# Four preactivated layers on 192x192x64: the input's shift and sums spread over three engines, and the weights of later layers prepared in later stages

## The reference, cut to what matters

```python
x = x + L0(gn(x))   # triangle multiplication
x = x + L1(gn(x))   # triangle multiplication
x = x + L2(gn(x))   # MLP with weights and activations rounded to fp8 by rows
x = x + L3(gn(x))   # triangle multiplication, masked
```

```python
h = (x - mu) * rsqrt(var + eps) * ln_w + ln_b
ab = fp8_linear(h, w1); a, b = split(ab)
out = fp8_linear(relu(a) * b, w2)
# fp8_linear: each row of x and of w is divided by max|row|/448 and rounded to fp8, the product is scaled back
```

## Time and profile before

| what | value |
|---|---|
| device time, median of 3 runs | 1818.19 us (1813.92 to 1819.84) |
| device time of the profiled execution | 1815.44 us |
| span of the profiled execution, first to last instruction | 1813.7 us |
| mean granted TensorE clock over the span | 0.913 of full speed |
| busy share of PE, DVE, ACT, POOL | 80%, 83%, 60%, 53% |
| start of the first group norm's reduction | 91.90 us |
| start of the group norm of layer 1, layer 2, layer 3 | 493.34, 898.61, 1440.2 us |

### The profile page before, as it was taken

How to read it: one execution, slowest core, us unless ns; L and a number is a source line. 1 busy time by engine, 2 the same in 40 slices (tenths; PEclk the granted TensorE clock), 3 DMA queues, 4 the chain that set the end, 5 groups by cost and what they waited for, 6 DMA issues and landing times.

```text
span 1813.7 us, 30465 instructions
## 1 busy us (share of the span) xinstructions
PE 1453.9 (80%) x9712; PEld 982.0 (54%) x9712; DVE 1503.7 (83%) x3826; ACT 1095.1 (60%) x2284; POOL 969.2 (53%) x665
## 2 busy tenths in 40 slices
PE   5569998899779997898899846666666489998765
PEld 1146666765456666765587613333333267767654
DVE  6889993398799992399689989999999699981588
ACT  2246662399646562399543367777777267771598
POOL 7378870187588870287555503333333488850354
PEclk8779999899979999899999958889899889999789
DMA  7024435277634435377544304344444434436377
GB/s 258 0 70 112 109 88 134 82 215 206 172 84 106 108 88 136 84 218 194 173 108 112 79 18 111 94 114 97 113 98 110 117 94 107 115 73 150 120 259 248
DMA packets 408831, 225.51 MB, mean 124 GB/s; under 512 B 343456, under 2 KB 343776, under 8 KB 408672
## 3 DMA queue, kind: packets, MB, share of 16 engines
q1 hardware_dynamic: 270240, 185.81, 37.4%
q10 hardware_dynamic: 138432, 37.76, 8.9%
HBM read 114.97 MB, written 66.06 MB: 100 GB/s over the span
## 4 chain that ended last, share of the span: by engine, by line
issue 32%; PE 31%; DVE 14%; ACT 11%; POOL 8%; DMA 3%; SPq 0%; ACTq 0%; POOLq 0%; DVEq 0%
PE ps L1145 11%; ACT work L992 8%; PE ps L1150 7%; PE ps L1106 5%; POOL work L518 4%; PE ps L1135 4%; PE ps L1225 4%; POOL work L472 3%; DMA gate_dram<-work 2%; DVE work L746 2%; ACT work L978 2%; DVE stats L804 2%; DVE work L634 1%; DVE tok L814 1%; DVE pairs L851 1%
## 5 line engine op out<-in xcount | busy, mean ns | idle before, releaser
L512 POOL TENSOR_TENSOR ln_s<-ln_s,half_power 128x8 f32<-128x8 f32 x216 | 358.7, 1661 | 358.9 <-DVE ln_s L728 306.1
L1106 PE MATMUL ps<-work,ones 128*128 128x512 f32 x504 | 281.6, 676 | 58.2 <-ACT work L954 48.4
L1145 PE MATMUL ps<-work 128*128 128x384 f32 x864 | 318.7, 492 | 2.1 <-ACT work L978 2.1
L1003 ACT ACTIVATE work<-ps 128x768 f32<-128x768 f32 x216 | 175.2, 811 | 170.3 <-DMA gate_dram<-work 128.2
L992 ACT ACTIVATE work<-pairs,ln_s 128x64 f32<-128x64 f32 x648 | 264.0, 502 | 19.1 <-DVE ln_s L735 19.1
L1150 PE MATMUL ps<-work 128*128 128x256 f32 x864 | 223.8, 382 | 0.0
L518 POOL TENSOR_TENSOR work<-pairs,work 128x512 f32<-128x512 f32 x36 | 75.9, 2108 | 273.6 <-DVE pairs L914 273.6
L1150 PEld LDWEIGHTS ps<-work 128*128 128x128 f32 x864 | 165.8, 192 | 69.8 <-issue 1.8
L1145 PEld LDWEIGHTS ps<-work 128*128 128x128 f32 x864 | 157.3, 192 | 67.2 <-ACT work L978 3.5
L746 DVE TENSOR_SCALAR work<-work,ln_s 128x64 f32<-128x64 f32 x468 | 189.9, 474 | 0.0
L1135 PE MATMUL ps<-ident,work 128*128 128x128 f32 x864 | 142.9, 291 | 53.8 <-DVE work L746 42.5
(11 more groups left out here) (149 smaller groups left out, 2805.5 us busy)
## 6 DMA issues: line engine op xcount, KB each, us to landing
work<-x_mid SPq DMA_DIRECT2D x144, 256.0 KB, 2.8
gate_dram<-work ACTq DMA_DIRECT2D x108, 256.0 KB, 3.1
work<-gate_dram SPq DMA_DIRECT2D x108, 256.0 KB, 3.1
work<-in_x_in SPq DMA_DIRECT2D x72, 256.0 KB, 2.8
work<-x_nat SPq DMA_DIRECT2D x144, 128.0 KB, 3.0
x_mid<-work SPq DMA_DIRECT2D x72, 256.0 KB, 2.6
work<-pairs SPq DMA_DIRECT2D x96, 96.0 KB, 3.0
work<-pairs ACTq DMA_DIRECT2D x96, 96.0 KB, 3.2
```

The costliest lines, as they stand in the source:

```text
L512: pool.tensor_tensor(ln_s[:, b, RSTD, :], ln_s[:, b, VAR, :], half_power[:, 0:U], ALU.pow)\
L1003: act.activation(sig[:, b, :].rearrange("p (k g) -> p k g", k=PAIRS)[:, 2 * half:2 * half + 2, :], ps[:, bank:bank + 2, 0:GATES], ACT.Sigm ...
L1106: last = pe.matmul(ps[:, bank, :], ones[:], src[:, b, :], start=first, stop=end, skip_group_check=True)
L1145: last = pe.matmul(ps[:, GATE_BANK[half] + k, 0:GATES], xnT[:, b, (2 * half + k) * P:(2 * half + k + 1) * P], wpair[:, VALUES:VALUES + GAT ...
```

## The change

Five things are changed.

1. **The shifts.** POOL subtracts the anchor from the even tiles only, DVE from the odd ones (`shifted_odd`).
2. **The sums.** Only the 24 tiles whose number is not a multiple of 3 (`ACC_TILES`) are added up by DVE, 23 additions; the other 12 are summed by PE directly, each with one more product with ones into the same PSUM bank as the last product with `acc`.
3. **The loads.** The second piece of the input (tiles 1 to 5) is loaded ahead of the parameters. The MLP's weights are no longer loaded at the start, but in layer 1 after its multiplication stage, behind a memset on POOL (`wq_cleared`).
4. **The weights.** In the input stage only layer 0's weights are scaled, in front of DVE's shifts. Their biases are folded after `group_norm(0)`. The weights of the two other triangle layers are scaled within `move_products` of layer 0, PE's products for them stand before layer 0's output stage, and their biases are folded after it. `quantise_weights` and PE's transposes stand between layer 1's output stage and `group_norm(2)`, `split_weights` after that group norm.
5. **Places.** `wbias` gets its own tensor, `sx_all` and three like it move into `pairs`, the unused bf16 identity is dropped.

The diff, cut to its core:

```diff
+ACC_TILES = [t for t in range(36) if t % 3]
-SUM_PARTS = [(0, 4), (4, 8), (8, 12), (12, 16), (16, 36)]
...
 # sync engine
+            load_whole(1)
             sp.dma_start(wfold[:], weights).then_inc(s_params, 16)
...
-            sp.wait_ge(s_const, 1)
-            sp.dma_start(wq_raw[:, 0:512], w1).then_inc(s_params, 16)
-            sp.dma_start(wq_raw[0:C, 512:768], w2).then_inc(s_params, 16)
+            for k in range(2, len(WHOLE)):
+                load_whole(k)
...
                     sp.wait_ge(chan_done, CHANNEL_PAIRS * BLOCKS * (q + 1))
+                    if l == 1:
+                        sp.wait_ge(wq_cleared, 1)
+                        sp.dma_start(wq_raw[:, 0:512], w1).then_inc(wq_loaded, 16)
+                        sp.dma_start(wq_raw[0:C, 512:768], w2).then_inc(wq_loaded, 16)
...
 # gpsimd
             for k, (lo, hi) in enumerate(WHOLE):
                 pool.wait_ge(x_whole[k], 16)
-                pipeline(pool, [(0, shift_input)], hi - lo, lo)
+                for t in range(lo, hi):
+                    if t % 2 == 0:
+                        shift_input(t)
...
+                    if l == 1:
+                        pool.wait_ge(chan_done, CHANNEL_PAIRS * BLOCKS * (q + 1))
+                        pool.memset(wq_raw[:, 512:768], 0.0).then_inc(wq_cleared, 1)
...
 # vector
-            dve.wait_ge(s_params, 16 * 7)
+            dve.wait_ge(s_params, 16 * 5)
             dve.tensor_scalar(mlp_wb[:, 0, :], mlp_wb[:, 0, :], ROOT_C, None, ALU.mult)
...
+            def scale_weights(q, tmp):
+                dve.tensor_scalar(tmp[:, 0:PROJ], wfold[:, q, 0:PROJ], nrm_d[:, q, 0:1], None, ALU.mult)
+                dve.tensor_scalar(tmp[:, PROJ:], wfold[:, q, PROJ:], nrm_d[:, q, 1:2], None, ALU.mult).then_inc(s_fold, 1)
                 dve.tensor_scalar(wfold[:, q, 0:PROJ], wfold[:, q, 0:PROJ], nrm[:, q, 0:1], ROOT_C, ALU.mult, ALU.mult)
                 dve.tensor_scalar(wfold[:, q, PROJ:], wfold[:, q, PROJ:], nrm[:, q, 2:3], ROOT_C, ALU.mult, ALU.mult).then_inc(s_fold, 1)
+            def fold_biases(q, bank, tmp, steps):
                 dve.wait_ge(s_fold_pe, q + 1)
+                dve.tensor_tensor(tmp, ps[:, bank, 0:PROJ + C], wbias[:, q, :], ALU.add).then_inc(s_fold, 1)
+                dve.wait_ge(s_fold, steps)
+                dve.scalar_tensor_tensor(out=wfold[:, q, :], in0=tmp, scalar=ROOT_C / C, in1=wfold[:, q, :],
                                          op0=ALU.mult, op1=ALU.add).then_inc(s_fold, 1)
...
+            scale_weights(0, fold_tmp[:, 0, :])
+            def shift_input(t):
+                dve.tensor_tensor(tokens(whole_tile(t)), tokens(whole_tile(t)), over_tokens(anchor[:]), ALU.subtract)\
+                    .then_inc(shifted_odd, 1)
+            def accumulate(n, t):
+                input_shifted(t)
+                if n == 1:
+                    input_shifted(ACC_TILES[0])
+                    dve.tensor_tensor(acc, whole_tile(ACC_TILES[0]), whole_tile(t), ALU.add).then_inc(input_acc, 1)
+                elif n:
+                    dve.wait_ge(input_acc, n - 1)
                     dve.tensor_tensor(acc, acc, whole_tile(t), ALU.add).then_inc(input_acc, 1)
+            for k, (lo, hi) in enumerate(WHOLE):
+                dve.wait_ge(x_whole[k], 16)
+                for t in range(lo, hi):
+                    if t % 2:
+                        shift_input(t)
+                    for n, late in enumerate(ACC_TILES):
+                        if late == t - 2:
+                            accumulate(n, late)
...
                 group_norm(l)
                 dve.wait_ge(gn_ready, l + 1)
+                if l == 0:
+                    fold_biases(0, 1, fold_tmp[:, 0, :], 4)
...
                         move_products(q, k)
+                        if l == 0 and k in (2, 4):
+                            scale_weights(k // 2, fold_ein[:, k // 2 - 1, :])
...
+                    if l == 0:
+                        for k in range(2):
+                            fold_biases(k + 1, 2 + k, fold_tmp[:, k, :], 10 + 2 * k)
+                    if l == 1:
+                        quantise_weights()
                 else:
+                    split_weights()
...
 # scalar: the Abs of quantise_weights moves behind layer 1's output stage
+            for t in range(TILES):
+                square_input(t, t % 2)
...
 # tensor
-            pe.wait_ge(s_const, 9)
+            pe.wait_ge(s_const, 6)
+            def sums_of_input(t, b):
+                pe.wait_ge(sq_ready, t + 1)
+                last = pe.matmul(ps[:, SQ, :], ones[:], squares[:, b, :], start=t == 0, stop=t == TILES - 1, skip_group_check=True)
+                if t not in ACC_TILES:
+                    last = pe.matmul(ps[:, SUM, :], ones[:], whole_tile(t), start=t == 0, stop=False, skip_group_check=True)
+                last.then_inc(sums_ready, 1)
+            for t in range(TILES):
+                sums_of_input(t, t % 2)
+                if t == 12:
+                    pe.wait_ge(s_fold, 2)
+                    sum_bias_products(1, fold_tmp[:, 0, :])
+            pe.wait_ge(input_acc, len(ACC_TILES) - 1)
+            pe.matmul(ps[:, SUM, :], ones[:], acc, start=False, stop=True, skip_group_check=True).then_inc(input_summed, 1)
...
 # tensor, before layer 0's output stage; transpose_weights() stands behind layer 1's, split_weights' parts are awaited in weighted()
+                    if l == 0:
+                        pe.wait_ge(s_fold, 9)
+                        pe.wait_ge(z_act, CHANNEL_PAIRS // 2 * BLOCKS)
+                        pe.wait_ge(z_dve, CHANNEL_PAIRS // 2 * BLOCKS)
+                        for k in range(2):
+                            sum_bias_products(2 + k, fold_ein[:, k, :])
```

More of the change, by code:

```diff
@@ L130, in build @@
         sig = part(work, 6144, U * 3 * C)
-        wbias = work[:, 9216:9216 + 3 * (PROJ + C)].rearrange("p (q e) -> p q e", q=3)
+        fold_ein = part(work, 6144, PROJ + C)
         wpair = work[:, 10368:10368 + 2 * (PROJ + C)]
@@ L246, in build @@
          mlp_out_ready, mres_loaded,
-         s_apart) = [sem(f"sem_{k}") for k in range(81)]
+         shifted_odd, wq_cleared, wq_loaded,
+         s_apart) = [sem(f"sem_{k}") for k in range(84)]
         x_loaded, gate_stored, xnew_stored, mres_loaded, qT_ready, hqT_ready = [
@@ new lines, in split_weights @@
+            def split_weights():
+                dve.wait_ge(s_quant_pe, 1)
+                n = 9
+                for bank, dst, width in ((2, w1s, 2 * HID), (3, w2s, 2 * C)):
+                    rest = w_rest[:, 0:width]
+                    n += 5
+                    chain(dve.tensor_copy(dst[:, 0, :], ps[:, bank, 0:width]), n - 4)
+                    chain(dve.tensor_tensor(rest, ps[:, bank, 0:width], dst[:, 0, :], ALU.subtract), n - 3)
+                    chain(dve.tensor_copy(dst[:, 1, :], rest), n - 2)
+                    chain(dve.tensor_tensor(rest, rest, dst[:, 1, :], ALU.subtract), n - 1)
+                    chain(dve.tensor_copy(dst[:, 2, :], rest), n)
@@ L638, in group_norm @@
+            for k, (lo, hi) in enumerate(WHOLE):
+                dve.wait_ge(x_whole[k], 16)
+                for t in range(lo, hi):
+                    if t % 2:
+                        shift_input(t)
+                    for n, late in enumerate(ACC_TILES):
+                        if late == t - 2:
+                            accumulate(n, late)
+            for n, late in enumerate(ACC_TILES):
+                if late >= TILES - 2:
+                    accumulate(n, late)
             def group_norm(l):
@@ L965, in square_input @@
                 act.activation(squares[:, b, :], whole_tile(t), ACT.Square).then_inc(sq_ready, 1)
-            for k, (lo, hi) in enumerate(SUM_PARTS):
-                pipeline(act, [(0, square_input)], hi - lo, lo)
-                if k == 0:
-                    act.wait_ge(s_quant, 5)
-                    act.activation(wq_magic, wq_y, ACT.Abs, scale=SPLIT).then_inc(s_quant_abs, 1)
+            for t in range(TILES):
+                square_input(t, t % 2)
             def evacuate_xnT(m, t, b, free_sem, free_value):
@@ L1080, in _ @@
                                    (3, lambda t, b, r: normalise(l, 1, xn_out, xn_transposed(1), t, b, r), RING)] + tail)
+                    if l == 1:
+                        act.wait_ge(s_quant, 5)
+                        act.activation(wq_magic, wq_y, ACT.Abs, scale=SPLIT).then_inc(s_quant_abs, 1)
                 else:
@@ new lines, in sum_bias_products @@
+            def sum_bias_products(bank, tmp):
+                pe.matmul(ps[:, bank, 0:PROJ + C], ones[0:C, :], tmp[0:C, :], start=True, stop=True).then_inc(s_fold_pe, 1)
+            for t in range(TILES):
[5 more added lines that the diff above has]
+            pe.matmul(ps[:, SUM, :], ones[:], acc, start=False, stop=True, skip_group_check=True).then_inc(input_summed, 1)
@@ L1128, in transpose_xn, with transpose_weights @@
+            def transpose_weights():
+                pe.wait_ge(s_quant, 9)
```

(5 more changed lines are left out.)

140 lines of the change are left out of this document (58 added, 82 removed).

## The result

| what | before | after |
|---|---|---|
| device time, median | 1818.74 us (4 runs) | 1796.37 us (4 runs, 1793.64 to 1799.89) |
| device time of the profiled execution | 1815.44 | 1793.64 |
| span of the profiled execution | 1813.7 | 1791.9 |
| mean granted TensorE clock | 0.913 | 0.919 |

The ratio is 0.9883, with a 95% interval of 0.9858 to 0.9909: 22.4 us or 1.2% faster. The forecast was 1798, its own range 1793 to 1804.

What follows compares the result with a forecast made beforehand. The prediction took the input stage to be bound by a DVE chain, 51 us of weights and 28 of additions. Its terms, -25 + 0.9 + 3.8 + 1.0 = -19.3, gave 1796.1 to 1798.9, taken as 1798 us, range 1793 to 1804.

Steps and rivals of the forecast that it cites:

- The input stage: Start to layer 0's group norm: weights moved out and work spread, its reduction moves from 91.90 to 67, minus 25 us.
- Layer 0's biases: After layer 0's group norm: DVE folds biases ahead of `pair_weights`, partly offset by shorter copies, +0.9 us.
- Scaling and folding for the other layers: Layer 0's multiplication stage and before layer 1's group norm: weight scaling and bias folding hidden in DVE's waits, 0 us.
- Quantising: Before layer 2's group norm: quantising the MLP weights outlasts DVE's 4.42 us of idle time and delays the reduction, +3.8 us.
- Splitting: After layer 2's group norm: ten DVE instructions take 4.3 us, slightly more than the idle 3.58, +1.0 us.
- Sum: Whole kernel: -25 + 0.9 + 3.8 + 1.0 = -19.3 us.
- A: Input stage and quantising: collisions cost DVE little, PE alone sets the stage at 64; -24.6 us, total 1793; chance 15%.
- B: Input stage: DVE and POOL wait out each other's whole instruction, stage ends at 72; -14.3 us, total 1803; chance 21%.
- C: Moved weight work: quantising +9, splitting +5.9, biases +1.7 at crowded prices; -8.4 us, total 1809; chance 9%.
- D: Input stage: PE, waiting tile by tile, stays at 1.2 GHz, 1.71 us a product; +13.3 us, total 1831; chance 5%.

Runs made afterwards that it cites:

- e3: Changed kernel, but DVE shifts all 36 input tiles and POOL none; first group norm's reduction at 60.96 us, single execution of 1786.48 us.
- e1: Changed kernel, but POOL shifts all 36 input tiles, DVE adds all 36, PE sums only squares; median 1802.67 us, 0.9903 of the kernel before.
- e2: Changed kernel's spread of shifts and sums, but all weights prepared in the input stage and loads in the old order; median 1819.76 us, ratio to before 1.0.
- e6: Changed kernel, but parameters loaded ahead of tiles 1 to 5 again; first group norm's reduction at 68.10 us, 68.66 when repeated; span 1789.9 us.

## Why the prediction was right

By its own steps:

**The input stage** (forecast minus 25, with the reduction at 67; measured 65.00 and 64.49, minus 26.9 and 27.4). Right in mechanism and nearly in size. DVE let go: 12.7, measured 12.84. DVE and POOL taking turns from 17.5 to 43.0 at 1.7: measured 17.52 to 42.68, 1.76 long and 1.68 from start to start. The start at 17.5 was partly luck: four instructions at 0.80 were put before it, and there were five at 0.60 with a wait of 0.35 for the transfer of tile 6. After that PE is the bound, as said. The surplus of 2 us comes from PE: it took 3.65 for three tiles (PE products from 20.66 to 24.31), 1.217 a tile and not 1.265 (one product after another is 0.86 from start to start; the 0.90 of the forecast had the tail of the last one in it), and at 43.6 it had 17 tiles left, where the forecast had 18 at 43. DVE's own end was put at 60.6 and came at 56.2, since an addition between two shifts has no gap: 0.60 from start to start, not 0.80. It was off the path, so nothing hung on it. e3 and e1 bear out the collision from both sides, by taking it away (-4.0) and by putting it on 30 of POOL's shifts instead of 15 (+5.7, with PE's direct sums undone too).

**Layer 0's biases** (+0.9). From L671 to the first L719 it was 4.68 before, from L710 to the first L758 5.15 after: +0.5. The copies of `pair_weights` became shorter, 2.11 for six instead of 3.47, because POOL had finished; the forecast had given that effect too little.

**Scaling and folding for the other layers** (0). Hidden. In the multiplication stage the next copy waited 3.62 instead of 4.53. Before the group norm of layer 1 DVE's idle time shrank from 4.42 to 1.26 and was not used up, though one of the four instructions met POOL and took 1.59. Layer 0's piece was 401.9 on average in the ten executions with these edits and 401.6 in the two without (before, e2).

**Quantising** (+3.8): +4.3. From the first of its instructions, 870.09, to the reduction at 878.85 it is 8.76, where DVE had been idle for 4.42. The first nine instructions took 4.0 instead of the 3.3 that were put down, L598 alone 1.13 beside POOL; POOL's weights were finished when the second half began, so the 0.4 of collision put down there did not come.

**Splitting** (+1.0): +0.94 at the first L843, ten instructions in 4.57 from 886.97 to 891.54. The whole of layer 2 did not become longer by it (541.6 and 541.6), so either it was made up later or the scatter, 540.6 to 543.6, hides it.

**Sum**: -26.9 + 0.5 + 4.3 + 0.9 = -21.2, forecast -19.3, measured in the spans -21.8. The term that was off most is the input stage, by 1.9.

**The rivals.** A (less collision) and B (more) bracketed it; the collision came near the size that L624 had shown (1.65 there, 1.76 here, 1.68 from start to start). The Trainium skill (SBUF — State Buffer, Who interferes with whom) calls the shared port pair an exclusive lock, and the trace agrees in kind: a pair takes nearly as long as the two instructions one after the other. It does not agree in size: both whole durations, an estimate by that rule, would be 1.93 a pair; 1.68 was measured. C fell: at crowded prices quantising would have cost 9, it cost 4.3. D, PE at its low clock, did not come in the changed kernel's input stage, where the granted clock was 1.00 from 20 us to the end, but it was not far: both executions of e6's load order showed it in small. Its 1.71 a product was read at 18.54 to 20.25, where the profile of before shows no clock of 0.50; PE's products between 50.60 and 52.31, at 0.50 in the earlier trace rows, have the same 1.71, so the price stands.

One piece stays open. Layer 1's interval grew by 5.9 in the first pair of profiles, of which quantising explains 4.3. The other 1.6 lies within the scatter of that interval, and no cause was isolated for it. The forecast had named 3 to 5 as the growth of this gap: the first pair's 5.9 lies outside, the 4.3 between the averages inside.

## What to carry to other kernels

When one engine's chain sets a stage, first take out of it what belongs to later stages; that, with the new load order, gave four fifths of the input stage's gain here, and spreading the rest before that would have given nothing. Before work is shared between DVE and POOL, look in a trace at what such an instruction takes beside the other engine's: here one with two SBUF inputs went from 0.68 to 1.76, and even the scaling of 64 values with one from 0.25 to 1.25. DVE alone did all 59 shifts and additions by 48.8 us, while with 18 of the shifts on POOL it was done at 56.2. Moved work is free where its engine waits for longer than it takes, so read the idle time before the next instruction at the new place, and prefer the stage with the widest gaps: quantising cost 4.3 us before the group norm and nothing that shows above the scatter in the multiplication stage.

## What the runs showed of the hardware

- Two engines that take turns do it at 1.68 us a pair, with DVE's 0.68 and POOL's 1.26 alone: 0.26 less than their sum. Part of that is overlap that each engine has with itself: undisturbed, DVE's follow each other every 0.60 and POOL's every 1.22, together 1.82, so the turns save 0.14 against that. The 1.68 held for 15 pairs in a row, and for 30 in e1.
- After a wait of PE of 2.2 us the granted clock fell from 1.00 (2.4 GHz) to 0.50 (1.2 GHz) in both executions of one load order, so that windows of 5 us around the fall show 0.79 to 0.86 on average. After the same wait it held at 1.00 in three executions of the other order, in which the wait ended 2 to 3 us sooner. From the end of that wait to the reduction it was 25.68 us in the first two and 24.76 in the other three, 0.9 more. The Trainium skill (TensorE: Matmul & The Clock Gate, HAM oscillation) warns of PE idling between bursts; the trace agrees in two of these five executions, and no run here shows what decides between them.
- In a stage that no experiment touched, layer 3, the length varied from 368.2 to 381.5 over twelve executions, and its mean granted clock between 0.946 and 0.889, on the whole the longer the lower. The longest had a granted clock of 0.53 in a stretch of 40 us in which the changed kernel had 0.90. A stage-by-stage comparison settles here what single whole times can't.
